# The two transfers per batch that place the transposed score maxima, issued by GpSimd instead of SyncE

## The chip, the cores and the metric

The kernel runs on one core of a Trainium2 chip. The metric is the device time of one execution in microseconds (us), the median of several runs. TensorE (PE) multiplies matrices, VectorE (DVE) reduces and combines, ScalarE (ACT) evaluates functions and copies, GpSimd (POOL) does elementwise work from on-chip memory, SyncE (SP) does nothing but issue transfers. They run unsynchronized and meet at semaphores. A transfer, by whichever engine it is issued, is carried out by the core's 16 DMA engines.

## The reference

Two transformer layers over x of 32 batches x 256 tokens x 128 features, each sublayer followed by a residual sum and a layer norm:

```python
x = layernorm(x + attention0(x))   # 16 heads of 8; q and v get a low-rank (LoRA) addition; full softmax
x = layernorm(x + moe(x))          # 8 experts, top 2, experts over capacity dropped
x = layernorm(x + attention1(x))   # 16 heads of 8; rotary positions; causal softmax
x = layernorm(x + spline_ffn(x))   # tokens routed to 64 small spline tables; own layer norm inside
# attention, of one batch and head:
#   softmax(q @ k.T * 8**-0.5) @ v, then all heads @ w_proj
```

All data are fp32.

## The kernel before

The four sublayers run one after another. The two attentions are one function, `attention`, called as `attn0` and `attn1`; they take from about 20 to 610 us and from about 680 to 1260 us. The change is in it alone.

**One batch.** x is transposed and projected to q and k (128 features on partitions: 8 features x 16 heads). The products of fp32 q and k are made in bf16: GpSimd splits q and k into three bf16 parts each (`parts`, L267 to L277, "the split"; in `attn1` the rotation by sine and cosine, L257 to L261, comes ahead of it). SP stores the parts to scratch memory in HBM (L204, L206) and loads them back as stacks of 72 rows for each head (`q_st`, `k_st`, six loads of 192 KB at L223, 24 rows of 8 KB each), so that one bf16 matmul over 72 rows sums all part products.

The scores are computed twice. `score_rows` (L535) puts queries on partitions; VectorE takes the maximum over the keys of each head (L353, `negmax`), splits it in a high and a low bf16 part (`split_max`, L364 and L366), and TensorE transposes them (`transpose_max`, L471); ScalarE copies the result from PSUM to `mT_sb` (L338 for heads 0 to 7, group 0; L309 for heads 8 to 15, group 1), 16 partitions x 256 bf16, 8 KB. **The transfer in question** places these 8 KB as two more rows, 72 and 73, under the stack of q for eight heads. `k_st` holds ones there. `score_cols` (L557, behind a mask matmul L553 in `attn1`) then puts keys on partitions and multiplies 74 rows, so that the maxima come off the scores by themselves; ScalarE takes the exponential (L297), and `sum_values` (L574) multiplies with v.

**The pipeline.** Each engine runs its own loop of steps over the batches, five deep, three steps to a loop pass (`pipeline`, three buffer slots). In a step the lag says which batch a piece belongs to: lag 0 is projected, split and stored, lag 2 has its row scores, lag 3 its column scores, lag 4 its projection and layer norm. TensorE, ScalarE and VectorE go through the 16 heads n = 0 to 15 of a step, column scores of lag 3 and row scores of lag 2 side by side, with the other work put at heads by the table `AT`. So group 0 of the maxima is copied at n = 11 of its own step and wanted at n = 0 of the next (`m_placed[0]`); group 1 is copied at n = 1 (`attn0`) or n = 0 (`attn1`) of the next step and wanted at its n = 8 (`m_placed[1]`). The q/k copy of ScalarE (L321, L324), which starts GpSimd's split, is one head behind the copy of group 1.

**The queues.** SP takes its step in this order: load x for the next batch (L186); place group 1 (L195); wait for the split and for the slot, then store the parts (L204, L206); place group 0 (L211); wait until the stores have landed and the column scores of the slot's former batch are through, then issue the six stack loads (L223). GpSimd's order: residual plus bias (L247, `attn0` only); rotation and split; the power that gives the reciprocal standard deviation (L282). ScalarE may copy new maxima over `mT_sb` only when the group's former transfer has landed.

`apart` is one increment of a semaphore that nothing waits for; it stands between two instructions.

Of the kernel before, what the change touches and what calls it, by code (L numbers as in the profile page):

```python
# [17 lines left out]
H, D = 16, 8  # L18
# [8 lines left out]
KROWS = PARTS * PARTS * D  # L27
MROWS = 2
K_BLOCK = PARTS
STORES, STACKS = 2, PARTS  # L30
NH = H // 2
# [38 lines left out]
def apart(eng, mem):  # L70

    eng.sem_inc(mem["apart"], 1)
# [22 lines left out]
def attention(nc, name, mem, causal, x_dram, lora, rope):  # L95
# [12 lines left out]
    with ExitStack() as ctx:  # L108
# [3 lines left out]
        def sem(label):  # L112
# [9 lines left out]
        q_st = sb("q_st", [P, SLOTS, H, N], BF16)  # L122
# [3 lines left out]
        mT_sb = sb("mT_sb", [MROWS * NH, 2, N], BF16)  # L126
# [25 lines left out]
        m_placed = [[sem(f"m_placed{g}{j}") for j in range(SLOTS)] for g in range(2)]  # L152
# [5 lines left out]
        xT_kept, qk_kept, v_kept, max_kept, mhi_kept, mparts_kept, mT_kept, probs_kept, oT_kept = (  # L158
            sem(x) for x in ("xT_kept", "qk_kept", "v_kept", "max_kept", "mhi_kept", "mparts_kept", "mT_kept",
                             "probs_kept", "oT_kept"))  # L160
# [18 lines left out]
        @block.sync  # L179
        def _(sp):  # L180
            def load_x(st, lag):

                wait(sp, xT_ready, st.seq(lag, c=1 - SLOTS))
                src = x_all[:, bass.ds(st.seq(lag, TB), TB), :] if x_dram is None else \
                    x_dram[:, bass.ds(st.seq(lag, TB), TB), :]
                sp.dma_start(x_in[:, st.slot(lag), :, :], src).then_inc(x_loaded[st.slot(lag)], 16)  # L186

            def step(st):
                if st.has(-1):
                    load_x(st, -1)  # L190
                if st.has(3):

                    sp.wait_ge(mT_kept, st.seq(3, 2, 2))
                    sl = st.slot(3)
                    sp.dma_start(q_st[KROWS:KROWS + MROWS, sl, NH:H, :], mT_sb[:, 1, :]).then_inc(m_placed[1][sl], 16)  # L195
                if st.has(0):
                    sl = st.slot(0)
                    sp.wait_ge(lo_kept, st.seq(0, c=1))
                    apart(sp, mem)

                    wait(sp, q_stacked[sl], st.turn(SLOTS, 16 * STACKS))
                    apart(sp, mem)
                    wait(sp, k_stacked[sl], st.turn(SLOTS, 16 * STACKS))
                    sp.dma_start(scratch[sl, 0:2 * PARTS].rearrange("b p n -> p b n"),  # L204
                                 parts[:, :, :, :].rearrange("p s j n -> p (s j) n")).then_inc(parts_stored[sl], 16)
                    sp.dma_start(scratch[sl, 2 * PARTS:K_BLOCK + 2 * PARTS - 1].rearrange("b p n -> p b n"),  # L206
                                 parts[:, 1, 0:PARTS - 1, :]).then_inc(parts_stored[sl], 16)
                if st.has(2):
                    sp.wait_ge(mT_kept, st.seq(2, 2, 1))
                    sl = st.slot(2)  # L210
                    sp.dma_start(q_st[KROWS:KROWS + MROWS, sl, 0:NH, :], mT_sb[:, 0, :]).then_inc(m_placed[0][sl], 16)  # L211
                if st.has(0):
                    sl = st.slot(0)
                    sp.wait_ge(k_ones, 1)
                    sp.wait_ge(parts_stored[sl], st.turn(0, 16 * STORES))
                    apart(sp, mem)

                    wait(sp, cols_ready, st.seq(SLOTS, H, H))

                    for j in range(PARTS):  # L220
                        rows = slice(PARTS * D * j, PARTS * D * (j + 1))
                        for stack, block, stacked in ((q_st, 0, q_stacked), (k_st, K_BLOCK + j, k_stacked)):
                            sp.dma_start(stack[rows, sl, :, :].rearrange("p h n -> p (h n)"),  # L223
                                         scratch[sl, block:block + PARTS].rearrange("a (d h) n -> (a d) (h n)", d=D))\
                                .then_inc(stacked[sl], 16)

            load_x(Step(0, 0, SLOTS, B), 0)
            pipeline(sp, step)

        @block.gpsimd  # L230
        def _(pool):
# [11 lines left out]
            def step(st):  # L243
                if st.has(4) and x_dram is not None:

                    wait(pool, y_kept, st.seq(4))
                    nc.gpsimd.tensor_tensor(x_res[:, :, :], x_all[:, bass.ds(st.seq(4, TB), TB), :],  # L247
                                            bo[:, :].unsqueeze(1).broadcast_to([P, TB, C]), ALU.add)\
                        .then_inc(x_res_kept, 1)
                if st.has(0):  # L250

                    pool.wait_ge(qk_kept, st.seq(0, QKOPS, QKOPS))
# [11 lines left out]
                    if st.has(1):  # L264
# [11 lines left out]
                    pool.wait_ge(mid_kept, st.seq(0, c=1))  # L276
                    nc.gpsimd.tensor_tensor(parts[:, :, 2, :], rest[:, :, :], parts[:, :, 1, :], ALU.subtract)\  # L277
                        .then_inc(lo_kept, 1)
                if st.has(4):

                    pool.wait_ge(var_kept, st.seq(4, c=1))
                    nc.gpsimd.tensor_tensor(rstd[:, :], var[:, :], mem["minus_half"][:, 0:TB], ALU.pow)\  # L282
                        .then_inc(rstd_kept, 1)
# [1537 lines left out]
```

## Time and profile before

| | us |
|---|---|
| median of 3 runs (1537.18 to 1553.59) | 1544.43 |
| the profiled execution | 1533.47 |
| its span on the core | 1531.7 |

The profile is of one execution, 11 us below the median. It shows each engine's busy time and, for each idle time, what ended it, inferred from the semaphores. An idle engine costs nothing unless it is the one that sets the pace. "PEclk" is the clock granted to TensorE as a share of full speed, "DMA" the mean busy share of the 16 DMA engines. Instructions that issue a transfer are listed as SPq, with the time the issue took. "PEld" is TensorE's loading of weights, the first thing a matmul needs of its stationary operand.

### The profile page before, as it was taken

Reading aid. Unit: us, or ns where it says so; the run is one execution under the profiler, and the core shown is the slowest. Engines: PE = TensorE matmul, PEld = TensorE weight load, DVE = VectorE, ACT = ScalarE, POOL = GpSimd, SP = SyncE. Lnnn points to the kernel's source line nnn. Section 1 sums busy time; section 2 is a strip of 40 time slices with the busy share of each in tenths; the row PEclk is TensorE's granted clock in tenths of the full one; section 3 lists DMA queues with packets and bytes.
Section 4 is the critical chain, followed back from the end, with each engine's and each line's share of the span. In section 5 each row is a group of like instructions: output and inputs, shape, how many; then the busy total and the mean of one; then the engine's idle time right before and its main releaser. Section 6 shows DMA issues by size and latency. Waiting matters only on the chain. (4 is left out here: it accounts for less than half of the span.)

```text
span 1531.7 us, 36081 instructions
## 1 busy us (share of the span) xinstructions
PE 1142.7 (75%) x11411; PEld 786.7 (51%) x11411; DVE 1102.7 (72%) x2949; ACT 845.0 (55%) x1844; POOL 552.9 (36%) x572
## 2 busy tenths in 40 slices
PE   2699998999999987415999999999999984402220
PEld 1355655655565654203677767777777752202220
DVE  1477888888888886723677677767777757798996
ACT  1265666666666665442666666666666653302555
POOL 5222332223222311354444454445445305002555
PEclk9998999999999999756999999999999997755555
DMA  5644544445444540305444444454445302000011
GB/s 139 155 103 98 117 110 111 97 114 112 113 97 113 113 94 2 118 17 135 98 109 113 115 101 108 114 113 99 111 113 114 94 2 76 35 0 0 29 34 48
DMA packets 115921, 137.26 MB, mean 90 GB/s; under 512 B 12112, under 2 KB 101520, under 8 KB 106640
## 3 DMA queue, kind: packets, MB, share of 16 engines
q1 hardware_dynamic: 112704, 132.25, 36.2%
q10 hardware_dynamic: 3152, 4.20, 1.0%
q8 instruction: 34, 0.56, 0.2%
q14 instruction: 31, 0.25, 0.1%
HBM read 85.03 MB, written 37.75 MB: 80 GB/s over the span
## 5 line engine op out<-in xcount | busy, mean ns | idle before, releaser
L353 DVE TENSOR_REDUCE attn_negmax<-attn_row_ps 128x2 f32<-128x512 f32 (+1 forms) x1024 | 609.7, 618 | 283.0 <-PE attn_row_ps L535 273.7
L297 ACT ACTIVATE attn_probs<-attn_col_ps 128x512 f32<-128x512 f32 (+1 forms) x1024 | 542.5, 547 | 299.3 <-PE attn_col_ps L557 282.2
L557 PE MATMUL attn_col_ps<-attn_q_st,attn_k_st 74*128 74x256 bf16 (+1 forms) x2048 | 373.2, 264 | 36.7 <-DMA attn_q_st<-attn_mT_sb 34.6
L535 PE MATMUL attn_row_ps<-attn_k_st,attn_q_st 72*128 72x256 bf16 (+1 forms) x2048 | 375.3, 266 | 16.1 <-DMA attn_k_st<-attn_scratch 15.2
L574 PE MATMUL attn_out_ps<-attn_probs,attn_v_sb 128*32 128x256 f32 (+1 forms) x4096 | 255.1, 368 | 1.3 <-ACT attn_probs L297 1.3
L557 PEld LDWEIGHTS attn_col_ps<-attn_q_st,attn_k_st 74*128 74x128 bf16 x2048 | 180.6, 99 | 131.8 <-ACT attn_probs L297 41.0
L535 PEld LDWEIGHTS attn_row_ps<-attn_k_st,attn_q_st 72*128 72x128 bf16 x2048 | 204.4, 100 | 44.3 <-issue 16.7
L282 POOL TENSOR_TENSOR attn_rstd<-attn_var,minus_half 128x2 f32<-128x2 f32 x64 | 45.4, 710 | 459.7 <-DVE attn_var L418 459.7
L531 PE MATMUL attn_row_ps<-mask_qk,ident_h 128*128 128x256 bf16 x512 | 141.9, 277 | 23.5 <-DMA attn_k_st<-attn_scratch 23.5
L553 PE MATMUL attn_col_ps<-mask_kq,ident_h 128*128 128x256 bf16 x512 | 142.0, 277 | 23.3 <-DMA attn_q_st<-attn_mT_sb 22.1
L574 PEld LDWEIGHTS attn_out_ps<-attn_probs,attn_v_sb 128*32 128x32 f32 x4096 | 108.9, 111 | 90.0 <-issue 25.0
L257 POOL TENSOR_TENSOR attn_q_half<-attn_q_half,sin 128x512 f32<-128x512 f32 x32 | 40.7, 1272 | 146.4 <-ACT attn_qk L324 146.2
L1524 POOL TENSOR_TENSOR ffn_rstd<-ffn_var,minus_half 128x8 f32<-128x8 f32 x19 | 31.9, 1679 | 167.3 <-DVE ffn_var L1546 167.3
L479 PE MATMUL attn_in_ps<-attn_xT,wqk 128*128 128x256 f32 x256 | 80.6, 442 | 1.8 <-ACT attn_xT L303 1.8
L553 PEld LDWEIGHTS attn_col_ps<-mask_kq,ident_h 128*128 128x128 bf16 x512 | 49.9, 97 | 61.7 <-DMA attn_q_st<-attn_mT_sb 25.1
L267 POOL TENSOR_SCALAR attn_parts<-attn_qk 128x512 bf16<-128x512 f32 x64 | 39.5, 618 | 113.6 <-ACT attn_qk L321 102.1
L1468 PE MATMUL ffn_r_ps<-ffn_table_hm,ffn_ohT 128*128 128x193 bf16 x64 | 21.0, 361 | 75.0 <-ACT ffn_ohT L1480 75.0
L277 POOL TENSOR_TENSOR attn_parts<-attn_rest,attn_parts 128x512 bf16<-128x512 f32 x64 | 74.3, 1162 | 5.4
L270 POOL TENSOR_TENSOR attn_rest<-attn_qk,attn_parts 128x512 f32<-128x512 f32 x64 | 74.0, 1156 | 5.4
L531 PEld LDWEIGHTS attn_row_ps<-mask_qk,ident_h 128*128 128x128 bf16 x512 | 49.6, 97 | 33.0 <-issue 24.2
L1457 PE MATMUL ffn_o_ps<-ident_h,ffn_onehot 128*128 128x128 bf16 x64 | 10.1, 313 | 73.4 <-PEq L1172 73.4
L1487 ACT ACTIVATE ffn_z<-ffn_y,ffn_shift,ffn_rstd 128x128 f32<-128x128 f32 x64 | 26.3, 482 | 55.5 <-DVE ffn_shift L1551 55.5
(229 smaller groups left out, 1694.5 us busy)
## 6 DMA issues: line engine op xcount, KB each, us to landing
attn_q_st<-attn_scratch SPq DMA_DIRECT2D x192, 192.0 KB
attn_k_st<-attn_scratch SPq DMA_DIRECT2D x192, 192.0 KB
attn_scratch<-attn_parts SPq DMA_DIRECT2D x64, 384.0 KB, 2.8
attn_scratch<-attn_parts SPq DMA_DIRECT2D x64, 128.0 KB, 2.8
attn_x_in<-in_L_attn_x_dram SPq DMA_DIRECT2D x32, 128.0 KB, 7.0
moe_xs<-x_all SPq DMA_DIRECT2D x8, 512.0 KB, 3.1
attn_x_in<-x_mid SPq DMA_DIRECT2D x32, 128.0 KB, 7.0
ffn_xs<-x_mid SPq DMA_DIRECT2D x16, 256.0 KB, 2.3
```

The costliest lines, as they stand in the source:

```text
L257: nc.gpsimd.tensor_tensor(q_half[:, :, :], q_half[:, :, :], sin, ALU.mult).then_inc(sin_done, 1)
L270: nc.gpsimd.tensor_tensor(rest[:, :, :], qk[:, :, :], parts[:, :, 0, :], ALU.subtract)\
L277: nc.gpsimd.tensor_tensor(parts[:, :, 2, :], rest[:, :, :], parts[:, :, 1, :], ALU.subtract)\
L282: nc.gpsimd.tensor_tensor(rstd[:, :], var[:, :], mem["minus_half"][:, 0:TB], ALU.pow)\
L297: nc.scalar.activation(probs[:, u % 2, j, 0:W], col_ps[:, n % 2, 0:W], ACT.Exp, scale=scale).then_inc(probs_kept, 1)
L353: nc.vector.tensor_reduce(negmax[:, t, 2 * p:2 * p + 2], row_ps[:, row_bank(st, u), 0:2 * keys].rearrange("p (a k) -> p a k", a=2), AX_X, ...
L479: last = nc.tensor.matmul(in_ps[:, s * N:(s + 1) * N], wqk[:, s, :], xT[:, st.slot(0), :], start=True, stop=True)
L531: nc.tensor.matmul(seen[:, :, keys - P:keys], ident_h[:, :], mask_qk[:, :, :], start=True, stop=False, skip_group_check=True)
L535: last = nc.tensor.matmul(bank[:, a * keys:(a + 1) * keys], q_st[0:KROWS, sl, h, t * P:(t + 1) * P], k_st[0:KROWS, sl, h, 0:keys], start=n ...
L553: nc.tensor.matmul(seen[:, :, 0:P], ident_h[:, :], mask_kq[:, :, :], start=True, stop=False, skip_group_check=True)
L557: last = nc.tensor.matmul(bank[:, t * N:(t + 1) * N - first], k_st[0:rows, sl, h, t * P:(t + 1) * P], q_st[0:rows, sl, h, first:N], start= ...
L574: last = nc.tensor.matmul(out_ps[32 * j:32 * j + 32, g * N + first:(g + 1) * N], v_sb[:, st.slot(lag), t, 32 * h:32 * h + 32], probs[:, u ...
```

## The change

SP loses two pieces of its step: placing group 1 (L195) and placing group 0 (L211), each with its wait for ScalarE's copy. GpSimd gains both. Group 1 stands behind the residual sum and ahead of the wait for the q/k copy, so ahead of the rotation and the split of the same step. Group 0 stands behind the split and ahead of the wait for the variance. Source, destination, size and semaphore of both are as before. No transfer was issued by GpSimd before.

```diff
--- before.py
+++ after.py
@@ -188,11 +188,6 @@
             def step(st):
                 if st.has(-1):
                     load_x(st, -1)
-                if st.has(3):
-
-                    sp.wait_ge(mT_kept, st.seq(3, 2, 2))
-                    sl = st.slot(3)
-                    sp.dma_start(q_st[KROWS:KROWS + MROWS, sl, NH:H, :], mT_sb[:, 1, :]).then_inc(m_placed[1][sl], 16)
                 if st.has(0):
                     sl = st.slot(0)
                     sp.wait_ge(lo_kept, st.seq(0, c=1))
@@ -205,10 +200,6 @@
                                  parts[:, :, :, :].rearrange("p s j n -> p (s j) n")).then_inc(parts_stored[sl], 16)
                     sp.dma_start(scratch[sl, 2 * PARTS:K_BLOCK + 2 * PARTS - 1].rearrange("b p n -> p b n"),
                                  parts[:, 1, 0:PARTS - 1, :]).then_inc(parts_stored[sl], 16)
-                if st.has(2):
-                    sp.wait_ge(mT_kept, st.seq(2, 2, 1))
-                    sl = st.slot(2)
-                    sp.dma_start(q_st[KROWS:KROWS + MROWS, sl, 0:NH, :], mT_sb[:, 0, :]).then_inc(m_placed[0][sl], 16)
                 if st.has(0):
                     sl = st.slot(0)
                     sp.wait_ge(k_ones, 1)
@@ -247,6 +238,11 @@
                     nc.gpsimd.tensor_tensor(x_res[:, :, :], x_all[:, bass.ds(st.seq(4, TB), TB), :],
                                             bo[:, :].unsqueeze(1).broadcast_to([P, TB, C]), ALU.add)\
                         .then_inc(x_res_kept, 1)
+                if st.has(3):
+                    pool.wait_ge(mT_kept, st.seq(3, 2, 2))
+                    apart(pool, mem)
+                    sl = st.slot(3)
+                    pool.dma_start(q_st[KROWS:KROWS + MROWS, sl, NH:H, :], mT_sb[:, 1, :]).then_inc(m_placed[1][sl], 16)
                 if st.has(0):
 
                     pool.wait_ge(qk_kept, st.seq(0, QKOPS, QKOPS))
@@ -276,6 +272,11 @@
                     pool.wait_ge(mid_kept, st.seq(0, c=1))
                     nc.gpsimd.tensor_tensor(parts[:, :, 2, :], rest[:, :, :], parts[:, :, 1, :], ALU.subtract)\
                         .then_inc(lo_kept, 1)
+                if st.has(2):
+                    pool.wait_ge(mT_kept, st.seq(2, 2, 1))
+                    apart(pool, mem)
+                    sl = st.slot(2)
+                    pool.dma_start(q_st[KROWS:KROWS + MROWS, sl, 0:NH, :], mT_sb[:, 0, :]).then_inc(m_placed[0][sl], 16)
                 if st.has(4):
 
                     pool.wait_ge(var_kept, st.seq(4, c=1))
```

## Rows read from the trace of the kernel before

**Rows 1.** Busy time by engine over the span, part 1 of the page.

```profile
PE 1142.7 (75%) x11411; PEld 786.7 (51%) x11411; DVE 1102.7 (72%) x2949; ACT 845.0 (55%) x1844; POOL 552.9 (36%) x572
```

**Rows 2.** TensorE's waits: 60 to 600 us, then 700 to 1260 us (total, times, longest).

```profile
PE attn_col_ps L557 <- DMA attn_q_st<-attn_mT_sb: 34.6, 29, 1.8
...
PE attn_row_ps L535 <- DVE attn_negmax L353: 0.9, 2, 0.4
...
PE attn_col_ps L553 <- DMA attn_q_st<-attn_mT_sb: 22.1, 29, 3.2
```

**Rows 3.** Who waited for L195's transfers (first two), and for L211's (us, times).

```profile
  PE attn_col_ps L557: 34.6, 29
...
  PE attn_col_ps L553: 15.4, 25
...
  PE attn_col_ps L553: 6.7, 4
```

**Rows 4.** Timeline, one batch, first attention: start, duration, engine, line [idle before].

```profile
302.72 0.34 ACT L338 COPY attn_mT_sb<-attn_in_ps 16x256 bf16<-16x256 bf16 x1
...
303.09 0.64 SPq L211 DMA_DIRECT2D attn_q_st<-attn_mT_sb  x1
...
305.65 0.21 PEld L557 LDWEIGHTS attn_col_ps<-attn_q_st,attn_k_st 74*128 74x128 bf16 x2
...
305.74 0.33 SPq L223 DMA_DIRECT2D attn_q_st<-attn_scratch  x1
...
308.11 0.36 ACT L309 COPY attn_mT_sb<-attn_fin_ps 16x256 bf16<-16x256 bf16 x1 [0.48 <-PE attn_fin_ps L471]
...
309.25 0.65 SPq L195 DMA_DIRECT2D attn_q_st<-attn_mT_sb  x1
...
314.48 0.40 SPq L204 DMA_DIRECT2D attn_scratch<-attn_parts  x1
...
315.74 0.39 PE L557 MATMUL attn_col_ps<-attn_q_st,attn_k_st 74*128 74x256 bf16 x2 [1.39 <-DMA attn_q_st<-attn_mT_sb]
...
323.99 0.33 SPq L223 DMA_DIRECT2D attn_q_st<-attn_scratch  x1
```

**Rows 5.** Windows: us, PE PEld DVE ACT POOL busy, PEclk, DMA share, GB/s.

```profile
304.40:304.60 0.20, 0.20 (x8) 0.11 (x12) 0.20 (x1) 0.20 (x1) 0.00 (x0) 1.00 0.13 33
...
309.00:313.00 4.00, 4.00 (x49) 2.77 (x50) 3.11 (x6) 3.38 (x7) 2.39 (x3) 1.00 0.82 168
314.80:315.00 0.20, 0.00 (x0) 0.00 (x0) 0.20 (x2) 0.00 (x0) 0.00 (x0) 1.00 0.03 5
```

**Rows 6.** Windows, same columns: attention stretches, two batches, the clock dip.

```profile
60.00:600.00 540.00, 493.87 (x4752) 318.79 (x4756) 438.94 (x1027) 351.30 (x719) 145.93 (x177) 0.97 0.45 103
309.25:327.16 17.91, 16.21 (x151) 10.14 (x149) 13.80 (x34) 11.13 (x23) 4.96 (x6) 0.90 0.45 101
327.16:343.54 16.38, 15.06 (x154) 9.96 (x152) 13.99 (x34) 11.12 (x24) 4.96 (x6) 1.00 0.49 113
316.80:320.30 3.50, 3.50 (x27) 1.60 (x26) 1.84 (x5) 1.39 (x4) 0.00 (x0) 0.52 0.14 37
760.00:1250.00 490.00, 470.96 (x5332) 350.63 (x5329) 352.92 (x956) 313.90 (x715) 217.32 (x218) 1.00 0.44 103
```

**Rows 7.** Timeline of GpSimd, same batch of the first attention.

```profile
306.90 0.73 POOL L247 TENSOR_TENSOR attn_x_res<-x_all,bo 128x256 f32<-128x256 f32 x1
310.30 0.62 POOL L267 TENSOR_SCALAR attn_parts<-attn_qk 128x512 bf16<-128x512 f32 x1 [2.67 <-ACT attn_qk L321]
```

**Rows 8.** Timeline, one batch of the second attention: maxima copied, weights of the first head.

```profile
903.64 0.36 ACT L338 COPY attn_mT_sb<-attn_in_ps 16x256 bf16<-16x256 bf16 x1
...
907.06 0.10 PEld L553 LDWEIGHTS attn_col_ps<-mask_kq,ident_h 128*128 128x128 bf16 x1
```

**Rows 9.** DMA issues: KB each, median us to landing; two small ones.

```profile
moe_gate_T<-in_L_ffn_gate_w_dram ACTq DMA_DIRECT2D x1, 4.0 KB, 4.4
...
prep_b_r<-in_L_attn_b_v_dram SPq DMA_DIRECT2D x1, 0.5 KB, 1.7
```

## The prediction

> **What bounds the kernel now.** I read the shares of busy time first: TensorE is the fullest engine, GpSimd with 36% the emptiest [rows 1], and the two attention stretches are 1200 us of the span. Then TensorE's waits, one list for each attention. In the first attention nearly all its idle time is one wait, L557 on the transfer that places the transposed maxima, 34.6 us in 29 waits; in the second it is L553 on the same transfer, 22.1 us in 29 [rows 2]. By the transfers' own lines, L195 (the second half of the heads) is what is waited for in 34.6 us and 15.4 us of it, L211 (the first half) in 6.7 us, all in the second attention [rows 3]. The work of TensorE sets a batch's pace, and these waits are the only holes in it worth naming.
>
> The timeline of one batch shows why L195 is late. ScalarE ends the copy of the maxima at 308.47. SP has been issuing the six stack loads since 305.74, then the load of x, and comes to L195 at 309.25 [rows 4]. That costs 0.8 us. More costly is the data: the six loads are 1.15 MB and keep the transfer engines at 0.82 of all 16 from 309 to 313; the last bytes trickle at 314.8 to 315.0, and TensorE, idle since 314.35, resumes at 315.74, 0.74 us behind the last bytes [rows 4, 5]. L195 issued itself 6.5 us before that release. L211 meets an empty machine: issued 303.09, most of its bytes move between 304.4 and 304.6 [rows 4, 5].
>
> The waits cost more than themselves. Two neighbouring batches of the first attention last 17.91 and 16.38 us, with stalls of 1.39 and 1.01 us. Of the 1.53 us between them 0.38 is stall and 1.15 goes with a granted clock that falls to 0.52 for 3.5 us right behind the longer stall [rows 4, 6]: the lower of TensorE's two levels, 1.2 instead of 2.4 GHz. Over 60 to 600 us the granted clock is 0.97, so 0.03 x 540 / 0.5 = 32 us at the low level, some 9 such dips, 9 x 1.15 = 10.5 us lost. In the second attention it is 1.00 [rows 6].
>
> **The change, part by part.** *Removed from SP:* two waits and two issues of 0.64 us a batch. SP's next step behind L211 is the stack loads. In the first attention they then wait for the last column scores (they start at 323.99) [rows 4], in the second for the stores, so neither moves. Price nothing; the cover is that a stack is read a whole batch later. The two increments that `apart` adds on GpSimd are signals, price nothing in its idle time. Behind L195 SP waits for the split's last part, until 314.48, again unmoved [rows 4].
>
> *L195 on GpSimd, ahead of the split.* GpSimd is idle from 307.63 to the split at 310.30, and the copy it now waits for ends at 308.47, so the issue has 1.8 us before it holds up the split [rows 4, 7]; the second attention leaves more. If it took longer, the split would be late by the excess, then SP's stores behind it, then the stack loads. The stores leave at 314.48 and the loads at 323.99 [rows 4], so several us of excess are covered. Price nothing. ScalarE makes this copy ahead of the q/k copy in its own order, so the wait holds nothing back that could have run.
>
> What it gains is a queue of its own. Issued at 308.5 and landing as L211 does plus something, about 2.8 us, it is there by 311.5 to 313 (the range for a share of the busy engines); the column scores want it at 314.35. So I take the 34.6 us and the 15.4 us of L195 as gone, and the clock dips with them: 60.5 us. The bounds: 0 and 60.5. I take the upper end because the other work of TensorE has almost no waits in the same lists (0.9 us on VectorE) [rows 2], and VectorE is busy 14.0 of 16.38 us [rows 6] and still has room at 15.4.
>
> *L211 on GpSimd, behind the split.* SP gets it going at 303.09, and the weights that need it load at 305.65 without a wait [rows 4]. From the end of the copy, 303.06, that leaves 2.59 us. Bytes done by about 304.7 [rows 5] plus 0.7 us for the release, as behind L195, makes some 2.3 us for SP. No row shows a transfer issued by GpSimd. Lower bound for its time from issue to release: SP's 2.3 us, no stall. Upper bound: the slowest small transfer of the trace, 4 KB in 4.4 us from ScalarE's queue, against 1.7 us for 0.5 KB from SP's [rows 9]; that gives a stall of 4.4 - 2.6 = 1.8 us. I take 2.8 us, nearer to the many small transfers: a new stall of about 0.3 us at the first head of each batch of the first attention, 32 x 0.3 = 10 us. In the second attention the copy ends at 904.00 and the weights load at 907.06 [rows 8]: 3.06 us, so 2.8 us fits. SP comes to L211 there only behind both stores, and its data only behind theirs; that is what the 6.7 us of L211 are [rows 3]. Of this queueing GpSimd saves the part at SP, and I take half, 3.5 us, as gone. Behind this issue GpSimd has only L282, whose variance comes later still in the same batch; the cover is the idle time before it.
>
> The Trainium skill bears on this price ("DMA: Bandwidth & Descriptors", Latency and other measured facts): the first byte comes after about 1 us from GpSimd and 0.6 us from SP. By that rule the excess would be 0.4 us instead of my 0.5, the new stall 0.2 us and the sum about 3 us better; no row here shows the GpSimd side. It also warns ("SBUF — State Buffer", the "DVE blocks DMA" trap) that VectorE in a two-port mode keeps GpSimd from writing descriptors. The long VectorE operations beside both issues are the reductions, which read PSUM, so by that rule nothing is added; no row here shows it.
>
> **Sum.** -34.6 -10.5 -15.4 -3.5 +10 = -54 us on the profiled execution, 1533.5 us, to about 1479.5. The median of the three runs shown is 1544.4, 11 us above it; on that scale 1490 us.
>
> **Rivals.**
> *A, the transfer rides no earlier.* All queues end in the same 16 engines. At 168 GB/s over 0.82 x 16 = 13 busy engines one 8 KB row of a stack takes 0.63 us [rows 5]. Each of two engines has 8 rows of 512 B to place. If each of these waits its turn behind one stack row, that is 5.1 us from about 310: landed at 315 and released at 316, where it is now. For it: the transfer is sixteen short rows on two engines (L211 takes 0.13 of 16) [rows 5], and they are what would alternate. Against: rows of one transfer may go together, and not all 16 engines are busy. Then no gain from L195, and 10 us lost at the first head: +0 to +20 us, 1544 to 1564. The Trainium skill ("Trainium Kernel Development and Optimization", Key Constraints) leans this way, saying that issuing from several engines saves only issue time; by that alone the gain would be the 0.8 us of L195's later issue, at most.
> *B, the wait of L211 takes the place.* At 4.4 us to release the new stalls are 1.8 us x 32 and 1.3 us x 32, 99 us, against 64 gained: +35, 1580 us [rows 9]. It turns into a loss beyond about 3.9 us. For it: the margin at 305.65 is thin. Against: all SP's small transfers land in about 2 us.
> *C, the gain is half taken back* by the next limit, VectorE or a shorter stall at the first head with dips of its own: -27 us, 1517 us. For it: VectorE would stand at 14.0 of 15.4 [rows 6]. Against: TensorE waits for it 0.9 us in all [rows 2].
>
> **Numbers.** Chances: forecast 0.56, C 0.12, A 0.17, B 0.15. About 1% is what a measurement of this kernel can tell. Faster: forecast and C, 0.68. Same: most of A and a little of B, 0.16. Slower: the rest, 0.16. The forecast's own range is 1470 (no new stall, 64 to 67 us gained, and the scatter of the runs) to 1512. To leave out no more than 2 in 10 it has to reach into A: 1470 to 1555, with B outside.
>
> **What the changed profile would show.** TensorE's waits of L557 and L553 on the transfer fall from 57 us to about 10 and move from the middle of a batch to its first head; the granted clock of the first attention rises to 0.99 or 1.00; its batches last 15.5 to 16 us. The split starts at most a few tenths later. If the middle wait stays, A is right; if a wait over 1 us stands at each first head, B. Wrong would also be a GpSimd issue of more than 2 us, or VectorE's reductions growing longer beside it.

## The result, and the profile after

| | before | after |
|---|---|---|
| median | 1539.73 | 1557.74 |
| lowest to highest | 1533.90 to 1553.59 | 1548.90 to 1583.78 |
| the profiled execution (its span) | 1533.47 (1531.7) | 1566.01 (1564.3) |

Times are of all 17 executions of each kernel, us. The ratio of the two is 1.0129, with a 95% interval of 1.0107 to 1.0151; it leaves out the longest run of after (1583.78), which counts as slow. The change costs 1.3%, some 18 to 20 us, where 54 us of gain were forecast. The profiled execution of after lies 8 us above its median and that of before 6 us below, so of their difference of 32.5 us some 14 are scatter between executions.

In the kernel after, line numbers have moved: L245 places group 1 and L279 group 0, both on GpSimd; L214 loads the stacks; L310 and L339 copy groups 1 and 0; L558 and L554 are the column scores. First the page of after: busy time by engine, and the two rows of TensorE's column scores (busy, mean ns | idle before them, and how much of it ended with the transfer).

```profile
PE 1158.1 (74%) x11411; PEld 789.7 (50%) x11411; DVE 1105.4 (71%) x2949; ACT 847.8 (54%) x1844; POOL 629.6 (40%) x700
...
L558 PE MATMUL attn_col_ps<-attn_q_st,attn_k_st 74*128 74x256 bf16 (+1 forms) x2048 | 377.2, 266 | 44.7 <-DMA attn_q_st<-attn_mT_sb 42.5
...
L554 PE MATMUL attn_col_ps<-mask_kq,ident_h 128*128 128x256 bf16 x512 | 142.8, 279 | 25.0 <-DMA attn_q_st<-attn_mT_sb 24.5
```

The wait that was to go has grown: 42.5 + 24.5 = 67.0 us against 34.6 + 22.1 = 56.7 [rows 2]. By the transfers' own lines in after (who waited, us and times; then from issue to landing), first those of L245, then of L279:

```profile
  PE attn_col_ps L558: 40.2, 29
...
  PE attn_col_ps L554: 21.4, 29
...
DMA to landing us min/median/max: 1.9/6.5/8.0
```

```profile
  PE attn_col_ps L554: 3.1, 3
  PE attn_col_ps L558: 2.3, 3
...
DMA to landing us min/median/max: 1.9/1.9/3.1
```

Group 0 on GpSimd does as forecast or better (5.4 us of waits, 6.7 before [rows 3]). Group 1 lands after 6.5 us, where 2.8 to 4.5 were forecast, and its waits rise from 50.0 us [rows 3] to 61.6. One batch of the first attention of after, from the timeline (start, duration, engine, line [idle before]):

```profile
299.52 0.31 SPq L214 DMA_DIRECT2D attn_q_st<-attn_scratch  x1
...
301.92 0.36 ACT L310 COPY attn_mT_sb<-attn_fin_ps 16x256 bf16<-16x256 bf16 x1 [0.50 <-PE attn_fin_ps L472]
...
302.98 0.59 POOL L245 DMA_DIRECT2D attn_q_st<-attn_mT_sb  x1 [1.55 <-ACT attn_mT_sb L310]
304.10 0.61 POOL L263 TENSOR_SCALAR attn_parts<-attn_qk 128x512 bf16<-128x512 f32 x1 [0.53 <-ACT attn_qk L322]
...
309.47 0.39 PE L558 MATMUL attn_col_ps<-attn_q_st,attn_k_st 74*128 74x256 bf16 x2 [1.23 <-DMA attn_q_st<-attn_mT_sb]
```

GpSimd issues at 302.98, 3.46 us behind the first stack load, and the split that follows is not held up. (The issue comes 0.70 us behind the end of ScalarE's copy, at 302.28, though GpSimd was idle; more on that below.) But TensorE is released 9.95 us after the first stack load was issued. In the kernel before that was 315.74 - 305.74 = 10.00 us [rows 4]. The release goes with the stack loads, and who issues the small transfer hardly moves it.

**The packets say why.** The trace holds a record of every packet that the 16 engines move, with its queue, start, duration and size, but not its engine. These are the ones of GpSimd's queue for this transfer (us of the span), with SP's rows beside them: those of the stacks, and those of the load of x (128 KB), which SP issued at 302.07, 0.9 us ahead of GpSimd:

```
304.54 to 304.81                     8 small packets of 32 and 4 B
308.01                               the last of the 144 stack rows (8192 B each) ends
308.57                               the last of the 256 rows of x (512 B each) ends
307.98, 308.32                       the data starts: two packets of 4096 B
308.29 ... 308.60                    the other 22 packets of 32 and 4 B, the last at 308.60
309.47                               TensorE released
```

The two packets of data, issued at 302.98, first move at 307.98, when the stack rows are through. Of the 31 batches of the first attention, 23 look like this one (7 of the others come below; the last has no loads beside it). In the 23 the first data packet starts 5.17 us behind the issue (median), and the last stack row ends at 5.02, the last row of x at 5.59. The last small packet comes at 5.8, right behind x's last row. Six loads of 24 rows are 144 rows of 8 KB; at about 0.63 us each, spread over 12 engines that is 12 rows each, 7.6 us. That it is 12 is inferred: 12 rows start together at the head of the burst (300.43 to 300.65), and 8 small packets, a pair each of four engines, pass already 1.5 us behind the issue. The small transfer doesn't take turns with the rows, it stands behind them.

**What is new is the form of the completion.** Section 3 of the page, queues with packets, MB and share; first of before, then of after:

```profile
q1 hardware_dynamic: 112704, 132.25, 36.2%
```

```profile
q1 hardware_dynamic: 110400, 131.20, 35.5%
...
q0 software_dynamic: 4096, 1.11, 0.5%
```

SP's queue lost 2304 packets with 128 transfers, 18 each: 16 rows of 512 B and 2 others, one on each of the two engines that L211's share of 0.13 of 16 points to [rows 5]. GpSimd's queue has 4096, 32 each, by their number two on every one of the 16 engines: one of 4096 B (on two of them) or of 32 B (on 14), and one of 4 B. So, read from these counts, SP's transfer is through when two engines are, GpSimd's when all 16 are. In 7 of the 30 batches from 69 to 578 us the data fell on engines that had no stack rows and was in place 1.8 to 2.1 us after the issue; the last small packet still came 5.2 to 6.0 us after it, behind the rows of stacks and of x on the others. The Trainium skill has both halves ("DMA: Bandwidth & Descriptors"). Under "Queues, rings and completion order" it says that the semaphore's increment lands only after every earlier write of that engine, across its queues; under "Why a DMA increments its semaphore by 16 and not by 1", that a transfer from GpSimd has all 16 engines report, whatever its shape, and one from SP only those that carry it. The packets here agree with both. They show more in one point: the data packets too did not start until the rows queued earlier on their engine were through.

**Where the time went.** In the two profiled executions the span grew by 32.6 us. Measured from the first to the last column scores, 15.9 us of it lie in the first attention and 8.2 in the second; the other 8.5 lie outside both, where nothing was changed. Of the 24 us, waits on the transfer are 10.3. More goes with the clock (windows of after: us, PE PEld DVE ACT POOL busy, PEclk, DMA share, GB/s):

```profile
60.00:600.00 540.00, 488.59 (x4596) 312.11 (x4594) 430.34 (x998) 341.56 (x695) 182.11 (x238) 0.95 0.46 103
760.00:1250.00 490.00, 467.73 (x5210) 345.69 (x5210) 347.27 (x936) 309.65 (x704) 258.60 (x280) 0.99 0.47 107
```

The granted clock was 0.97 and 1.00 [rows 6]. The trace's own records of the clock are finer than these two places: in the first window the lower level was granted for 37.5 us in before and 51.2 in after, in the second for none and 8.8. These 22.5 us are 6.6 dips of 3.4 us, by the prediction's own measure 6.6 x 1.15 = 7.6 us. Together 10.3 + 7.6 = 18 of the 24 us; the other 6 are not accounted for. (That 18 is also the difference of the medians is chance, since the medians are of other executions.) Over the releases of the first attention the median distance from the first stack load is 9.86 us in before and 10.00 in after, and the longest in steady running 10.5 and 11.5. That the later part comes from the 16 completions is inferred, from the packets above and from e8 below, not shown for each batch.

### The profile page after: what moved, and what is told of

It reads as the page before. It is cut to its first block and busy times, and to the rows that moved or that the text cites. A ratio compares the mean times of both kernels' runs of the same rounds, so it can differ in the third digit from the quotient of the medians.

```text
span 1564.3 us, 36209 instructions
## 1 busy us (share of the span) xinstructions
PE 1158.1 (74%) x11411; PEld 789.7 (50%) x11411; DVE 1105.4 (71%) x2949; ACT 847.8 (54%) x1844; POOL 629.6 (40%) x700
## 3 DMA queue, kind: packets, MB, share of 16 engines
q0 software_dynamic: 4096, 1.11, 0.5%
## 5 line engine op out<-in xcount | busy, mean ns | idle before, releaser
L558 PE MATMUL attn_col_ps<-attn_q_st,attn_k_st 74*128 74x256 bf16 (+1 forms) x2048 | 377.2, 266 | 44.7 <-DMA attn_q_st<-attn_mT_sb 42.5
L536 PE MATMUL attn_row_ps<-attn_k_st,attn_q_st 72*128 72x256 bf16 (+1 forms) x2048 | 380.7, 269 | 16.6 <-DMA attn_k_st<-attn_scratch 15.7
L575 PE MATMUL attn_out_ps<-attn_probs,attn_v_sb 128*32 128x256 f32 (+1 forms) x4096 | 258.7, 372 | 1.3 <-ACT attn_probs L298 1.3
L558 PEld LDWEIGHTS attn_col_ps<-attn_q_st,attn_k_st 74*128 74x128 bf16 x2048 | 182.1, 100 | 141.7 <-issue 39.6
L554 PE MATMUL attn_col_ps<-mask_kq,ident_h 128*128 128x256 bf16 x512 | 142.8, 279 | 25.0 <-DMA attn_q_st<-attn_mT_sb 24.5
L279 POOL DMA_DIRECT2D attn_q_st<-attn_mT_sb x64 | 39.1, 611 | 296.2 <-ACT attn_mT_sb L339 296.0
L283 POOL TENSOR_TENSOR attn_rstd<-attn_var,minus_half 128x2 f32<-128x2 f32 x64 | 45.7, 714 | 142.7 <-DVE attn_var L419 142.7
L245 POOL DMA_DIRECT2D attn_q_st<-attn_mT_sb x64 | 37.7, 589 | 136.3 <-ACT attn_mT_sb L310 136.3
L554 PEld LDWEIGHTS attn_col_ps<-mask_kq,ident_h 128*128 128x128 bf16 x512 | 49.9, 98 | 65.8 <-DMA attn_q_st<-attn_mT_sb 26.7
```

The costliest lines, as they stand in the source:

```text
L536: last = nc.tensor.matmul(bank[:, a * keys:(a + 1) * keys], q_st[0:KROWS, sl, h, t * P:(t + 1) * P], k_st[0:KROWS, sl, h, 0:keys], start=n ...
L554: nc.tensor.matmul(seen[:, :, 0:P], ident_h[:, :], mask_kq[:, :, :], start=True, stop=False, skip_group_check=True)
L558: last = nc.tensor.matmul(bank[:, t * N:(t + 1) * N - first], k_st[0:rows, sl, h, t * P:(t + 1) * P], q_st[0:rows, sl, h, first:N], start= ...
L575: last = nc.tensor.matmul(out_ps[32 * j:32 * j + 32, g * N + first:(g + 1) * N], v_sb[:, st.slot(lag), t, 32 * h:32 * h + 32], probs[:, u ...
```

## The experiments

The theory that the runs left standing is called F: a small transfer is released only when what was queued before it on the same engines is written, whichever engine issued it, and what is queued later doesn't delay it. "On the same engines" is inferred throughout from times and counts of packets, since the records name no engine. Its rivals are named in the expectations. Each ratio is to the kernel before on the same chip. Edits are against the kernel before, unless "after" is said.

### Which transfer, and which engine

**e9_group1, e6_group0: one part of the change alone.** Only the first, or only the second, of the two pieces of the diff goes to GpSimd.

> The other part alone: group 1 on GpSimd ahead of the split, group 0 as before on SyncE behind the stores. My theory: the release stays behind the end of the stack loads and comes some tenths later than from SyncE's queue, because on GpSimd's queue the completion is reported by all 16 engines, the last of them being the one that sets it; with it more clock dips. It carries the whole loss: slower by 1 to 1.5%. Rival (SyncE's order is what costs, now that it reaches the stack loads without the wait for group 0): within 0.5% of before.

> One part of the change alone: group 0 on GpSimd behind the split, group 1 as before on SyncE ahead of the stores. My theory: group 0 lands in 2.0 to 2.6 us on an empty machine, makes no new wait at the first head worth naming and saves a little of its wait in the second attention; time within 0.5% of before. Rival (the whole of the change's loss comes from here, by the later landing of group 0): slower by over 1%.

Group 1 alone: 1565.57 us, ratio 1.0153 (1.0076 to 1.0230). Group 0 alone: 1538.81, 1.0003 (0.9963 to 1.0043). The source lines of group 1 alone (L249):

```profile
  PE attn_col_ps L557: 43.1, 29
...
  PE attn_col_ps L553: 24.2, 26
...
DMA to landing us min/median/max: 1.9/6.7/8.1
```

Within the intervals the whole loss is group 1's, with nearly the same landing as in after (6.7 us for 6.5). Group 0 has 5.8 us of waits (5.0 and 0.8) and lands in 2.0 us, for nothing gained or lost.

**e2_act: group 1 on ScalarE's queue.**

```diff
                             .then_inc(mT_kept, 1)
+                        act.wait_ge(mT_kept, st.seq(3, 2, 2))
+                        sl = st.slot(3)
+                        act.dma_start(q_st[KROWS:KROWS + MROWS, sl, NH:H, :], mT_sb[:, 1, :])\
+                            .then_inc(m_placed[1][sl], 16)
```

> The kernel before with group 1 issued by ScalarE right behind its own copy, so in a second hardware queue; group 0 stays with SyncE. Theory A1 (each 512 B row of the transfer takes its turn behind one 8 KB stack row on its two engines, whatever the queue): landing stays near 6 us, the wait at the middle head stays at 50 us or more in all, time within 1% of before or up to 1% slower for the issue on ScalarE. Rival A2 (what is late on GpSimd's queue is the completion, which all 16 engines have to report there, against two here): landing falls to about 3 us, the wait at the middle head falls under 10 us, time about 1485 us. Rival A3 (nothing but the queue's own order matters): as A2.

1538.83 us, ratio 1.000 (0.9961 to 1.0040). The timeline of one batch:

```profile
298.57 0.33 SPq L218 DMA_DIRECT2D attn_q_st<-attn_scratch  x1
...
301.34 0.62 ACTq L308 DMA_DIRECT2D attn_q_st<-attn_mT_sb  x1
...
308.43 0.39 PE L556 MATMUL attn_col_ps<-attn_q_st,attn_k_st 74*128 74x256 bf16 x2 [1.24 <-DMA attn_q_st<-attn_mT_sb]
```

Issued 2.77 us behind the first stack load (3.51 on SP [rows 4]), and released 9.86 us behind it (median of all batches 9.8, for 9.9 in before). The issue is 0.7 us earlier and the release is not, or by under 0.1 us. The wait in the first attention is 30.7 us for 34.6. In the second, L308 is waited for 1.9 us where L195 was 15.4 [rows 3], but TensorE's list has a new wait of 16.5 us on ScalarE's q/k copy, which now stands behind the issue. That is also why the waits on the transfer are 41 us in all, group 0's 8.4 among them, and not the 50 that the expectation had. In the first attention a third queue gives the same release, so it isn't something of GpSimd's queue that makes it late.

**e3_four_rows: one row a turn.** After, with a quarter of group 1: 4 rows of 512 B instead of 16. The kernel leaves out the other maxima (zeros, set once, stand in their place).

```diff
-                    pool.dma_start(q_st[KROWS:KROWS + MROWS, sl, NH:H, :], mT_sb[:, 1, :]).then_inc(m_placed[1][sl], 16)
+                    pool.dma_start(q_st[KROWS:KROWS + 1, sl, NH:NH + 4, :], mT_sb[0:4, 1, :]).then_inc(m_placed[1][sl], 16)
```

> The changed kernel, with group 1's transfer cut to 4 rows of the 16 (the high part of four heads; the other rows hold zeros, set once at the start by VectorE while it is idle), so 4 rows on one engine instead of 8 on each of two. The maxima of the other heads are left out of the exponent. Theory A1 (turns behind 8 KB rows, one per row): landing falls from 6.5 us to about 2 + 4 x 0.6 = 4.4 us, the wait at the middle head falls from 61 us to under 15 us, time about 1500 us. Rival A2 (the completion from all 16 engines is late): landing stays at 6 us or more and the wait stays near 60 us, time as the changed kernel.

1551.25 us, ratio 1.0056 (1.0010 to 1.0102). The source line of this transfer (L246):

```profile
  PE attn_col_ps L560: 36.1, 29
...
  PE attn_col_ps L556: 18.9, 26
...
DMA to landing us min/median/max: 1.6/6.6/7.6
```

A quarter of the data lands no earlier, 6.6 us for 6.5. The packets: the four of 512 B start at 322.17 to 322.41 in a batch issued at 317.34, on the heels of the last stack rows (322.30). In rival A of the prediction eight short rows of one engine each waited one turn. The expectation put all four rows on one engine; the packets are 4 of 512 B and 28 of 4 B, which reads as one row on each of four engines. A single row waits as long as eight, so turns are not what it waits for. In after there are no eight turns at all: the data are two packets of 4096 B.

### What goes ahead of it

**e1_ahead: SP places group 1 ahead of the stack loads** instead of behind them. No GpSimd, no new queue.

```diff
-                if st.has(3):
-
-                    sp.wait_ge(mT_kept, st.seq(3, 2, 2))
-                    sl = st.slot(3)
-                    sp.dma_start(q_st[KROWS:KROWS + MROWS, sl, NH:H, :], mT_sb[:, 1, :]).then_inc(m_placed[1][sl], 16)
...
+                if st.has(2):
+                    apart(sp, mem)
+                    sp.wait_ge(mT_kept, st.seq(2, 2, 2))
+                    sl = st.slot(2)
+                    sp.dma_start(q_st[KROWS:KROWS + MROWS, sl, NH:H, :], mT_sb[:, 1, :]).then_inc(m_placed[1][sl], 16)
+                if st.has(0):
+                    sl = st.slot(0)
                     for j in range(PARTS):
```

> The kernel before with one step moved: SyncE places group 1 of the maxima ahead of the six stack loads of the step before it, so the loads wait until ScalarE has copied the maxima (about 2.7 us later than now). Theory (the wait at the middle head is made by the stack loads that share the transfer engines): the transfer meets empty engines and lands about 2.3 us after its issue, the column scores' wait on it falls from 57 us to under 5 us, the granted clock of the first attention rises from 0.97 to 0.99 or more, and the kernel gains the 60 us summed in the prediction: about 1480 us. Rival (the wait only moves, to the row scores waiting for stacks that come 2.7 us later, or to VectorE): the wait on the transfer goes and the total stays within 1% of 1540 us.

1470.09 us, ratio 0.9563 (0.9485 to 0.9641). Nobody waits for group 1 (L219); for group 0 (L206) the waits, and then the window of the first attention, are:

```profile
  PE attn_col_ps L555: 9.2, 20
...
  PE attn_col_ps L559: 0.4, 1
```

```profile
60.00:560.00 500.00, 481.14 (x4820) 317.03 (x4820) 441.25 (x1046) 352.48 (x727) 148.07 (x180) 0.99 0.49 112
```

This is the gain that was forecast for taking group 1's waits away, 70 us for 60.5: the waits and the clock dips were sized about rightly, and what was wrong is by what they go away. (Counted in the profiles, e1 has 47 us less of waits on the transfer and 38 us less at the lower clock, 11 dips or 13 us; that is 60 of the 68 us that its two attentions are shorter. As above, some us go uncounted.) The stack loads, now behind a wait for the copy, cost nothing; the cover that the prediction named (a stack is read a batch later) holds.

**e5_stacks_held: all six stack loads wait until group 1 has landed.** After, with one wait on SP ahead of the loads: `sp.wait_ge(m_placed[1][st.slot(2)], st.turn(2))`.

> The changed kernel, with SyncE holding all six stack loads until group 1, issued by GpSimd, has landed. Theory F (what is queued before it on the transfer engines is all that makes it late): alone on the machine it lands in 1.9 to 2.1 us, the wait at the middle head is gone, the loads start about 5 us later than in the changed kernel and are still there in time; 1470 to 1485 us. Rival (GpSimd's queue itself is slow for this transfer): landing stays over 4 us even on an empty machine, or the time stays above 1530 us.

1534.44 us, ratio 0.9944 (0.9911 to 0.9977). Group 1 (L249) lands in 1.9 us and has no waits. But group 0 (L283) has, and the stack loads of this timeline suggest why:

```profile
  PE attn_col_ps L562: 32.0, 24
...
  PE attn_col_ps L558: 18.1, 31
...
DMA to landing us min/median/max: 1.9/3.0/5.3
```

```profile
313.80 0.31 SPq L218 DMA_DIRECT2D attn_q_st<-attn_scratch  x1
...
315.78 0.36 SPq L218 DMA_DIRECT2D attn_k_st<-attn_scratch  x1
...
318.07 0.38 SPq L199 DMA_DIRECT2D attn_scratch<-attn_parts  x1
```

The loads now leave 2 to 4 us ahead of the stores, the stores land later (longest 7.7 us for 6.1, median 3.5 for 2.8), and group 0, which is issued behind them, stands in the same queue of bytes. Of the 13 batches from 200 to 408 us, four had their last stack row done about 2 us ahead of group 0's issue, and it landed in 1.9 us; nine had it 0.3 to 1.1 us behind the issue, and it took 3.1 to 4.4. A time of 1470 to 1485 us was expected and missed: the mechanism was right for group 1 and was not followed on to group 0.

**e7, e8, e11: only the later loads held.** SP waits, ahead of the third pair of loads (four ahead) or the second pair (two ahead), until the issue is out. With ScalarE's queue in e7, with GpSimd's in e8 and e11; the issuing engine adds 1 to `sent` behind its issue, and in e11 the line has `j == 1`.

```diff
                     for j in range(PARTS):
+                        if j == 2 and st.has(2):
+                            apart(sp, mem)
+                            sp.wait_ge(sent, st.seq(2, c=1))
```

> As the run with group 1 on ScalarE's queue, but SyncE sends only the first four of the six stack loads ahead; the last two wait for a signal that ScalarE gives right behind its issue. In the runs so far the transfer was released 9.9 us behind the first stack load whatever queue it came from. Theory F (a transfer is released only when the bytes that were queued before it on the same engines have been written, across queues; what is queued later doesn't matter): release falls by the time of two loads, 2 x 192 KB at 160 GB/s = 2.4 us, and x's load no longer counts, so about 3.5 to 4.5 us from issue to release against 7.0, the wait at the middle head goes, about 1480 us. Rival T (it takes turns with rows of whatever is queued, earlier or later, until the traffic is over): release and wait as in the run with all six ahead, about 1540 us.

> The changed kernel, with the last two of the six stack loads held until GpSimd has issued group 1. Theory F: landing of group 1 falls from 6.5 us to about 4 us, the wait at the middle head from 61 us to under 10 us, about 1485 us, the granted clock of the first attention back to 0.99. Rival T: landing stays at 6.5 us and the time at that of the changed kernel.

> The changed kernel with only the first two stack loads ahead of group 1's issue on GpSimd, the other four held until then (four ahead gave a landing of 5.6 us, six 6.5 us). Theory F with a delay of about 1 us between GpSimd's issue and its rows entering the engines' queues, in which SyncE's next two loads slip in ahead: landing about 4.5 us, between 4 and 5. Rival T (turns with all traffic): 6 us or more. Rival F without the delay: about 2.5 us.

| | us | ratio | waits for group 1, both attentions | landing, median |
|---|---|---|---|---|
| e7, ScalarE, four ahead | 1491.00 | 0.9674 (0.9582 to 0.9766) | 1.3 | |
| e8, GpSimd, four ahead | 1498.92 | 0.9725 (0.9629 to 0.9822) | 8.9 + 2.5 | 5.6 |
| e11, GpSimd, two ahead | 1486.86 | 0.9634 (0.9565 to 0.9703) | none | 4.0 |

With e5 and the kernel after this is a dose, all on GpSimd's queue: none, two, four, six loads ahead give a landing of 1.9, 4.0, 5.6, 6.5 us. (The load of x stands ahead only with six; in the held runs SP issues it later.) What is left over e1 is in part group 0, which now meets more traffic: its waits are 11.1, 16.4 and 18.9 us in e7, e8 and e11, for 9.6 in e1, and e7 has 19.2 us on ScalarE's q/k copy besides. On ScalarE's queue the packets show the dose without GpSimd's form of completion. One batch of each:

```
     issue by ScalarE    its rows move          last stack row ends
e2   301.34              306.97 to 307.33       307.17
e7   311.99              314.22 to 314.67       317.46
```

In e7 the rows go 2.2 us behind the issue, not 5.6, while the two loads issued behind them (312.70 and 313.04) have nearly 3 us to go; the middle head's first matmul starts at 317.76 without a wait. So it isn't the end of all traffic that releases, which is the rival of F: what is queued later doesn't hold it. e8 was to land in about 4 us and took 5.6. Its line:

```profile
  PE attn_col_ps L562: 8.9, 18
...
DMA to landing us min/median/max: 1.9/5.6/6.6
```

The packets of one batch of e8 (issue 305.25, release 311.03) split it up: the two data packets start at 306.54 and 306.56, and the last small packet of the other engines at 310.01. SP's two loads, let go by the same signal, were issued at 305.27 and 305.60, and GpSimd's packets appear only 1.3 us behind its issue, so on the engines without its data the loads got in ahead. In this batch the data was in place some 3 us before the last of the reports. ScalarE's transfer, of which the packet counts (18) say that only two engines report, had 1.3 us of waits in the same place. The form of completion is the likeliest reason for the 11.4 against 1.3 us of waits, though the two runs also differ in the instant of the issue.

**e4_rows_4k: shorter stack rows.** After, with each stack load cut in two of 96 KB (rows of 4 KB, twelve issues).

```diff
+                            for g in range(2):
+                                sp.dma_start(stack[rows, sl, NH * g:NH * (g + 1), :].rearrange("p h n -> p (h n)"),
+                                             scratch[sl, block:block + PARTS].rearrange(
+                                                 "a (d h) n -> (a d) (h n)", d=D)[:, NH * N * g:NH * N * (g + 1)])\
+                                    .then_inc(stacked[sl], 16)
```

> The changed kernel with each stack load cut in two by heads: twelve loads with rows of 4 KB instead of six with rows of 8 KB, the same bytes. Theory A1: a turn costs half, so the transfer of group 1 lands after about 2 + 8 x 0.3 = 4.4 us instead of 6.5, its wait falls from 61 us to under 15 us, time about 1500 us. Rival (the transfer waits for the whole of the loads' bytes, not for rows): landing stays at 6 us or more, the wait stays near 60 us, time as the changed kernel or slower by SyncE's six more issues.

1487.72 us, ratio 0.9671 (0.9570 to 0.9772). Group 1 (L247):

```profile
  PE attn_col_ps L560: 2.1, 3
...
  PE attn_col_ps L556: 0.6, 1
...
DMA to landing us min/median/max: 1.9/4.7/6.1
```

Taken alone this run speaks for the turns of rival A: rows half as long, an earlier landing. But twelve issues last 4.8 us on SP (314.11 to 318.90 in one batch), and GpSimd's issue falls at 317.58, ahead of the last of them and of the load of x. The packets of this batch: the data starts at 320.75, the last small packet at 321.08, and the last stack row ends at 322.37, so some rows were let pass, those issued later. That fits F, and e3 speaks against the turns; what the 4 KB rows themselves are worth isn't separated from it.

### The best version, and group 0 again

**e12_ahead_again, e10_ahead_g0pool.** e12 is e1 once more, with more rounds; e10 is e1 with group 0 on GpSimd as well, behind the split as in after.

> The kernel with group 1 ahead of the stack loads on SyncE's queue again, unchanged, beside the one above on the same chip: 1465 to 1475 us, 4 to 5% faster than the kernel before. It is the measure for the run above: a gain of under 0.3% between the two can't be told from none.

> The kernel with group 1 placed ahead of the stack loads by SyncE (1470 us in its first run), and group 0 moved to GpSimd as in the change. Theory: in the second attention SyncE reaches group 0 only behind the stores, which left 9 us of waits at the first head; GpSimd sends it without that, so the waits fall to 2 to 4 us and the kernel gains 0.2 to 0.4%: about 1466 us. Rival (group 0 from GpSimd lands 0.2 to 0.3 us later and takes back what it gains, more so now that batches are shorter): the same or up to 0.5% slower than the run beside it.

e12: 1469.09 us, ratio 0.9518 (0.9476 to 0.9560). e10: 1480.27, 0.9598 (0.9556 to 0.9640). The waits for group 0 in e12 (L206), then in e10 (L281):

```profile
  PE attn_col_ps L555: 10.2, 19
```

```profile
  PE attn_col_ps L556: 15.2, 30
  PE attn_col_ps L560: 3.8, 6
DMA to landing us min/median/max: 1.9/2.6/3.1
```

GpSimd was to save the part of group 0's wait that SP's order makes, and it adds instead: 19.0 us for 10.2, and 0.8% of time, more than the rival had either. The issues show a cost that belongs to GpSimd: in every batch of after, e5, e6 and e10 it starts them 0.70 us or more behind the end of ScalarE's copy, where SP, when free, and ScalarE start theirs 0.03 us behind it. In the second attention SP starts group 0 1.21 us behind the copy in e12 (median) and GpSimd 0.71 in e10, so half a us is saved there, but the transfer then takes 2.9 us to land (1.9 in the first attention). What makes the 0.70 us, the wait itself, the increment of `apart` or the start of an issue, no run separates. Neither piece of the change is worth having. Moving one block within SP's own step is, and it gives 4.8%.

## Why the prediction was wrong

- **What bounds the kernel: right.** TensorE, and in it the wait on group 1. e1 and e12 take the wait away and give 69 and 74 us on the medians; the terms of the sum were 34.6 + 10.5 + 15.4 = 60.5. The clock goes with the waits as reasoned: with them gone the granted clock is 0.99, with more of them 0.95, and in e9 0.92.
- **"Removed from SP ... price nothing": right.** The stores leave 8.65 us behind the first stack load in the batch shown (299.52 to 308.17), for 8.74 in before [rows 4].
- **The issue on GpSimd, hidden: right, though it starts later than assumed.** It takes 0.59 us; the split starts at 304.10, 0.28 us behind the end of the q/k copy at 303.82. "Issued at 308.5" put it right at the copy's end, and it comes 0.70 us behind. VectorE's reductions were not longer beside it (619 ns mean for 618).
- **"What it gains is a queue of its own ... it is there by 311.5 to 313": the step that failed.** The term -60.5 became +18 in waits and dips. The transfer landed after 6.5 us instead of 2.8 to 4.5, because it stands behind the bytes that SP has queued on the engines, the stacks and x. The view for it had been read: L195's release comes just behind the last bytes of that traffic [rows 4, 5], in a queue where L195 was the last in order. This was taken for the order of SP's queue, and it is the order of the engines behind all queues. Nothing in the trace of before told the two apart, since no queue but SP's was in use in its attentions, and the range of the term (0 to 60.5) said so; the choice of its upper end had no row behind it. Its other end should also have lain beyond 0, for a queue whose completion was unknown.
- **Rival A, 1544 to 1564: nearest in time, wrong in mechanism.** It has the transfer ride no earlier, but by turns behind single rows, and it books the loss at the first head. e3 refutes the turns, and the loss is at the middle head, in waits on group 1 that grew by 11.6 us. The first head has 2.3 us, not 10.
- **"A new stall of about 0.3 us" for group 0: too large.** The term +10 came out as 2.3 us. Counted from the end of the copy, as the prediction did, it is 0.70 + 1.9 = 2.6 us for 2.8 taken, just about the margin of 2.59; rival B (4.4 us) is further off. (Its 4.4 us are not the slowest small transfer of the trace, as was said: `x_all` from ScalarE's queue, 0.5 KB, took 9.8. Nothing hung on it.) The 3.5 us gained in the second attention came out as 3.6 (6.7 to 3.1).
- **Rival C** (VectorE the next limit) has no support, but what spoke against it was misread. "TensorE waits for it 0.9 us in all" leaves out a row of the same list of before, the wait of `transpose_max` for VectorE's split of the maxima:

```profile
PE attn_fin_ps L471 <- DVE attn_mparts L366: 8.1, 29, 0.5
```

  With it, and 0.8 us at L471 for group 0, VectorE made TensorE wait 9.8 us. In e1, with the other waits gone, this row reads 8.0 us and the list is otherwise as before, so VectorE did not become the limit.
- The rule that issuing from several engines saves only issue time, which the prediction had from the Trainium skill ("Trainium Kernel Development and Optimization", Key Constraints), was weighed as "by that alone the gain would be the 0.8 us" and given the lesser chance. It was right in direction, and the runs on three queues agree with it (+1.3%, 0.0% and the kernel before itself); the loss of 1.3% it doesn't give.

## What to carry to other kernels

A small transfer that is waited for and issued into a burst of bulk loads isn't freed by another queue: here its time was set by the bytes queued on the engines before it. Put it ahead of the burst, or hold back the burst (or the later part of it) until it is issued, and then follow the burst to what it now runs into. A transfer from GpSimd also waited for engines that carry none of its data, and was issued 0.7 us later behind what it waited for, so a latency-bound one is better placed on SP or ScalarE, if their order allows it (in e2 it didn't: 16.5 us of waits on the q/k copy).

## What the runs showed of the hardware

- As far as times show it, an engine worked off packets in order of arrival over the queues: where the data of GpSimd's queue met SP's rows, it started 5.17 us behind the issue (median of 23 batches), with the last stack row ending at 5.02 us. With four of six loads ahead ScalarE's rows moved 2.2 us behind the issue (e7), with all six 5.6 us (e2).
- A transfer of 8 KB from GpSimd is 32 packets over all 16 engines, from SP 18 over two. Its issue takes 0.59 us, on free engines its first packet moves 1.2 us behind the issue (median of e5) and it lands in 1.9 us. The same transfer from SP moves first 1.3 us behind its issue of 0.64 us (before, 303.09 to 304.37), a stack load 0.9 us (299.52 to 300.43).
- GpSimd began an issue 0.70 us behind the end of the copy that it waited for (0.69 to 0.72 in the 64 issues of L245), SP, when free, and ScalarE 0.03 us (before L211, e2 L308).
- Data in place and data reported can be 3 to 4 us apart: 7 of 30 batches of after had the data by 2.1 us and the last completion at 5.2 us or later.
- From the last packet to TensorE's start it takes 0.86 us with GpSimd (308.61 to 309.47) and 0.90 with SP (314.84 to 315.74), in one batch each, so the report itself isn't slower.
